# A Perceiver kernel: nine key chunks of the third cross-attention made in the stages ahead of it, kept in DRAM and reloaded

## What is computed

```
k_raw = ctx @ wk_x[g].T                       # 6272 x 128
k     = layernorm(k_raw) * w + b              # mean and variance over the 128
p     = softmax(q[g] @ k.T / sqrt(128))
mix   = p @ ctx                               # 64 x 256 for each head
out   = mix @ wv_x[g].T
```

## Time and profile before

| | |
|---|---|
| median of 3 runs | 1033.47 us (1030.02 to 1033.73) |
| span of the profiled execution | 1029.9 us |
| its own time | not on the page; the lowest run is 1030.02 us |
| PE, DVE, ACT, POOL busy | 981.5, 715.1, 359.1, 162.3 us |
| mean granted TensorE clock | 0.991 |
| HBM read, written | 62.54 MB, 0.07 MB |

### The profile page before, as it was taken

One profiled execution on the slowest core, in us unless ns is written; L12 is line 12 of the kernel. 1 busy time (PEld: TensorE's weight loads), 2 busy tenths in 40 slices (PEclk: granted clock), 3 DMA queues, 4 the chain that ended last, 5 costly groups with the idle time before them and its releaser, 6 DMA issues.

```text
span 1029.9 us, 20637 instructions
## 1 busy us (share of the span) xinstructions
PE 981.5 (95%) x7832; PEld 655.9 (64%) x7848; DVE 715.1 (69%) x1916; ACT 359.1 (35%) x629; POOL 162.3 (16%) x146
## 2 busy tenths in 40 slices
PE   9999999998799888999999999999999999898998
PEld 5676677675335444566777777777777777744555
DVE  5767767768799845886676867667676867843444
ACT  2333333334338832432333332433333332302211
POOL 0000000000210010342223223222332323000000
PEclk9999999999999999999999999999999999898999
DMA  8001001002239996940000000000000000232440
GB/s 311 25 22 42 21 20 38 23 5 84 73 115 195 190 337 250 338 170 1 1 1 1 1 0 0 0 0 0 0 0 0 0 1 2 82 144 82 159 192 4
DMA packets 66410, 75.41 MB, mean 73 GB/s; under 512 B 49329, under 2 KB 57265, under 8 KB 62513
## 3 DMA queue, kind: packets, MB, share of 16 engines
q1 hardware_dynamic: 66064, 74.57, 23.7%
q10 hardware_dynamic: 288, 0.07, 0.0%
HBM read 62.54 MB, written 0.07 MB: 61 GB/s over the span
## 4 chain that ended last, share of the span: by engine, by line
PE 77%; DVE 8%; issue 6%; DMA 3%; POOL 2%; ACT 2%; SPq 0%; POOLq 0%; DVEq 0%; PEld 0%; PEldq 0%
PE ps L2377 17%; PE ps L2271 15%; PE ps L2367 8%; PE ps L1570 8%; PE ps L1560 4%; PE ps L1581 4%; PE ps L1604 2%; PE ps L1616 2%; POOL x_sum L2902 1%; PE ps L515 1%; DVE vals L2097 1%; PE ps L2989 1%; PE ps L2294 1%; DMA wide<-vals 1%; PE ps L1590 1%
## 5 line engine op out<-in xcount | busy, mean ns | idle before, releaser
L2377 PE MATMUL ps<-vals,S 128*128 128x257 f32 x784 | 188.3, 384 | 0.7 <-ACT S L2834 0.7
L2271 PE MATMUL ps<-keysT,row_biases_sb 128*128 128x512 f32 (+1 forms) x416 | 185.4, 572 | 0.1
L2902 POOL TENSOR_TENSOR x_sum<-x_max,consts 128x4 f32<-128x4 f32 (+1 forms) x104 | 135.3, 1301 | 316.2 <-DVE x_max L2570 316.2
L2582 DVE SCALAR_TENSOR_TENSOR S<-ps,x_sum,keysT 128x128 f32<-128x128 f32 x392 | 110.9, 345 | 66.4 <-PE ps L2377 61.8
L2377 PEld LDWEIGHTS ps<-vals,S 128*128 128x128 f32 x784 | 143.1, 192 | 18.9 <-issue 1.0
L2834 ACT ACTIVATE S<-S 128x512 f32<-128x512 f32 (+1 forms) x104 | 62.6, 605 | 219.8 <-DVE S L2623 219.3
L2367 PE MATMUL ps<-x_q,x_keys 128*128 128x128 f32 x784 | 113.2, 286 | 0.0
L2271 PEld LDWEIGHTS ps<-keysT,row_biases_sb 128*128 128x128 f32 x416 | 75.9, 191 | 56.9 <-issue 51.0
L2367 PEld LDWEIGHTS ps<-x_q,x_keys 128*128 128x128 f32 x784 | 95.6, 191 | 0.1
L1570 PE MATMUL ps<-ring,S 128*128 128x512 f32 x196 | 92.3, 593 | 0.1
L2766 ACT COPY x_keys<-ps 128x512 f32<-128x512 f32 (+1 forms) x104 | 57.0, 548 | 65.4 <-PE ps L2367 32.8
(11 more groups left out here) (474 smaller groups left out, 1374.6 us busy)
## 6 DMA issues: line engine op xcount, KB each, us to landing
ring<-weights SPq DMA_DIRECT2D x24, 1024.0 KB, 7.0
keysT<-ctxT SPq DMA_DIRECT2D x2, 3136.0 KB, 14.9
vals<-ctxN SPq DMA_DIRECT2D x1, 6272.0 KB, 27.0
S<-ctxT SPq DMA_DIRECT2D x11, 512.0 KB, 4.0
ring<-weights SPq DMA_DIRECT2D x5, 768.0 KB, 5.9
keysT<-weights SPq DMA_DIRECT2D x1, 1792.0 KB, 8.9
keysT<-weights SPq DMA_DIRECT2D x1, 1536.0 KB, 12.1
row_biases_sb<-row_biases SPq DMA_DIRECT2D x1, 1416.0 KB, 9.4
```

Of the source, the lines that this page charges most:

```text
L2271: ins = pe.matmul(ps[:, x2_key_bank(g, c), 0:width(c)], x2_wk[:, k, :], ctxT[:, k, span(c)], start=k == 0, stop=k == KT - 1)
L2377: ins = pe.matmul(bank(6, D + 1), S[:, a:a + TILE], ctx_and_ones[:, SUB * c + s, :], start=c == 0 and s == 0, stop=c == NC - 1 and s == su ...
L2582: ins = dve.scalar_tensor_tensor(S[:, a:a + TILE], ps[:, 3 + c % 2, 128 * s:128 * s + 128], x2_inv[:, c % 2, s:s + 1], x2_tile_const, ALU. ...
L2902: pool.tensor_tensor(x2_inv[:, c % 2, 0:n], x2_var[:, c % 2, 0:n], C("neg_half").broadcast_to([128, n]), ALU.pow)\
```

## The change

`KEPT` names nine chunks of 512 tokens: chunks 3, 5, 7, 9 and 11 of group 1 and 3, 5, 7 and 9 of group 7. Their raw keys are made before stage 6, each as four pieces (`keep(pe, n)` issues n pieces; a piece is one f32 matmul over 256 columns, two records), and the pieces take the places of the dummy matmuls in x0 to f1. ScalarE copies a finished chunk to a free part of the tile `S` (`copy_kept`), SyncE stores it to a DRAM tensor (`store_kept`, 256 KB) and brings it back in stage 6 (`load_kept`) into the slot of `x2_keys` where the copy of stage 6 put it. Eight of the nine take their context from five extra loads of 512 KB (`load_kept_ctx`) into `x2_keys` and `x2_probsT`, which are free then; the ninth takes it from `ctxT`. The key weights of both groups are loaded early into the end of ring slot 2, and VectorE centres them in the sweep (`centre_kept_weights`).

```diff
+KEPT = ((1, 3), (GROUPS - 1, 3), (1, 5), (GROUPS - 1, 5), (1, 7), (GROUPS - 1, 7), (1, 9), (GROUPS - 1, 9), (1, 11))
+KEPT_LOADS = ((0, 3), (1, 5), (0, 7), (1, 9), (1, 9))
+KEPT_LOAD_OF = (0, 0, 1, 1, 2, 2, 3, 4, None)
+KEPT_LOAD_DONE = (0, 0, 2, 4, 7)
...
+        def keep(pe, n):
+            for piece in range(kept_pieces[0], kept_pieces[0] + n):
+                u, (half, k) = piece // 4, divmod(piece % 4, KT)
...
+                if piece % 4 == 0:
...
+                    if u >= 2:
+                        pe.wait_ge(sem("kept_copied"), since("kept_copied", u))
+                    if load is None:
+                        pe.wait_ge(sem("ctxT_in"), 16 * KT)
+                    else:
+                        pe.wait_ge(sem(f"kept_ctx{KEPT_LOADS[load][0]}"), since(f"kept_ctx{KEPT_LOADS[load][0]}", 16 * kept_load_no(load)))
...
+                ins = pe.matmul(ps[:, KEPT_BANK[u], a:a + TWO], kept_weights[:, KEPT_GROUPS.index(g), k, :], source,
+                                start=k == 0, stop=k == KT - 1)
...
+        def copy_kept(act, u):
+            if kept_units:
+                act.wait_ge(sem("kept_psum"), since("kept_psum", u + 1))
...
+                act.copy(scratch(KEPT_AT[u], CHUNK), bank(KEPT_BANK[u])).then_inc(sem("kept_copied"), 1)
+        def centre_kept_weights(dve):
...
+            link(dve, "dve", dve.tensor_reduce(mean, kept_weights_flat, AX, ALU.add))
+            link(dve, "dve", dve.tensor_scalar(mean, mean, 1.0 / GD, None, ALU.mult))
+            dve.tensor_tensor(kept_weights_flat, kept_weights_flat, spread(mean, 2, GD), ALU.subtract).then_inc(sem("kept_weights"), 1)
...
+        KEPT_NORM = {1: 4, 2: 4, 3: 4, 4: 3, 5: 4} if kept_units else {}
...
-            if n in BUSY_NORM:
+            if n in KEPT_NORM:
+                keep(pe, KEPT_NORM[n])
+            elif n in BUSY_NORM:
                 busy(pe, *BUSY_NORM[n])
```

SyncE's order gains, in the first loads, two weight loads and two context loads ahead of the sweep's own context loads, and in `load`:

```diff
+                if name == "f0_up":
+                    store_kept(sp, 0)
+                    load_kept_ctx(sp, 2)
+                    store_kept(sp, 1)
+                if name == "f0_routed":
+                    store_kept(sp, 2)
+                    load_kept_ctx(sp, 3)
+                    store_kept(sp, 3)
+                if name == "f0_down":
+                    store_kept(sp, 4)
                 if name == "f1_lora":
+                    store_kept(sp, 5)
+                    store_kept(sp, 6)
...
+                    if kept_units:
+                        sp.wait_ge(sem("x1_scores_psum"), since("x1_scores_psum", PARTS * PAIRS))
+                    load_kept_ctx(sp, 4)
                     reload_ctxT(sp)
+                if name == "f1_experts0":
+                    store_kept(sp, 7)
                 if name == "f1_experts3" and runs(6):
...
+                    store_kept(sp, 8)
+                if name == "x2_proj1" and kept_units:
+                    kept_stored(sp, len(kept_units))
+                    sp.wait_ge(sem("x2_first_in"), 16)
+                    for u in kept_order:
+                        load_kept(sp, u)
```

In stage 6 a kept chunk has no `keys`, and its scores wait for the reload. The reload waits for the scores of the chunk that used the slot before. ScalarE skips the copy, squares from `x2_keys` and does so behind the exponential:

```diff
+        def load_kept(sp, u):
+            g, c = kept_units[u]
+            sp.wait_ge(sem("x2_scores_psum"), since("x2_scores_psum", g * NC + (c - 1)))
+            sp.dma_start(x2_keys[:, c % 2, :], kept_keys[u]).then_inc(sem("x2_kept_in"), 16)
...
-                        if c + 3 < NC:
+                        if c + 3 < NC and not kept(scored, c + 3):
                             keys(scored, c + 3)
...
-                    if scored is not None and c + 2 < NC:
+                    ahead_kept = scored is not None and c + 2 < NC and kept(scored, c + 2)
+                    if scored is not None and c + 2 < NC and not ahead_kept:
                         copy_keys(scored, c + 2)
                         square(scored, c + 2)
                     if weighed is not None and c + 2 < NC:
                         exp(weighed, c + 2)
+                    if ahead_kept:
+                        square(scored, c + 2)
```

More of the change, by code:

```diff
@@ L521, in perceiver @@
         transposed_no = {n: k for k, n in enumerate(transposed)}
+        kept_units = KEPT if first == 0 and last >= 6 else ()
+        kept_order = sorted(range(len(kept_units)), key=lambda u: kept_units[u])
+        kept_keys = nc.dram_tensor("kept_keys", (len(KEPT), 128, CHUNK), F32).ap()
+        kept_weights = ring[:, 2, SLOT - 512:SLOT].rearrange("p (g k n) -> p g k n", g=2, k=KT)
+        kept_weights_flat = cut(ring[:, 2, SLOT - 512:SLOT], 4, GD)
+        kept_ctx = [cut(x2_keys[:, :, :].rearrange("p a n -> p (a n)"), KT, CHUNK),
+                    cut(x2_probsT[:, :, :].rearrange("p a n -> p (a n)"), KT, CHUNK)]
@@ new lines, in kept_stored, with load_kept_ctx @@
+        def kept_stored(eng, units):
+            for s in range(2):
+                n = len([u for u in range(units) if u % 2 == s])
+                eng.wait_ge(sem(f"kept_stored{s}"), since(f"kept_stored{s}", 16 * n))
+        def load_kept_ctx(sp, i):
+            if kept_units:
+                place, c = KEPT_LOADS[i]
+                if i >= 2:
+                    sp.wait_ge(sem("kept_psum"), since("kept_psum", KEPT_LOAD_DONE[i]))
+                sp.dma_start(kept_ctx[place], io["ctxT"][:, :, span(c)]).then_inc(sem(f"kept_ctx{place}"), 16)
@@ L603, in out_tensor @@
             k = outs.index(s)
-            if s in BUSY_OUT:
+            if s == 0 and kept_units:
+                keep(pe, 4)
+            elif s in BUSY_OUT:
                 busy(pe, *BUSY_OUT[s])
@@ L705, in mha_tensor @@
             if s in mha_by_rows:
-                busy(pe, BUSY_MHA[s][0], 4)
+                if s == 4 and kept_units:
+                    keep(pe, 1)
+                    busy(pe, BUSY_MHA[s][0] - 2, 4)
+                else:
+                    busy(pe, BUSY_MHA[s][0], 4)
                 pe.wait_ge(sem("mha_qk_ready"), mha_by_rows.index(s) + 1)
@@ L722, in mha_tensor @@
             for c in range(2):
-                if not meanwhile:
+                if s == 1 and kept_units:
+                    keep(pe, 2)
+                elif not meanwhile:
                     busy(pe, BUSY_MHA[s][2], 4)
@@ L1795, in sweep_vector @@
                         norm_vector(dve, 0)
+                if i == 1 and kept_units:
+                    centre_kept_weights(dve)
             pair_step(2 * (NC - 1), 0, subs(NC - 1))
@@ L1840, in x0_tensor, with while_waiting @@
         def x0_tensor(pe):
-            busy(pe, 2, 3)
+            def while_waiting():
+                if kept_units:
+                    keep(pe, 1)
+                else:
+                    busy(pe, 2, 3)
+            while_waiting()
             norm_tensor(pe, 0)
-            busy(pe, 2, 3)
+            while_waiting()
             normT_here(pe, 0)
@@ L1978, in x1_tensor @@
             ins.then_inc(sem("x1_q_psum"), 1)
-            busy(pe, 9, 3)
+            if kept_units:
+                keep(pe, 4)
+            else:
+                busy(pe, 9, 3)
             for i in range(2):
@@ L2133, in x1_vector @@
             for b in range(PARTS):
+                if b == 1 and kept_units:
+                    kept_stored(dve, 6)
+                if b == PARTS - 1 and kept_units:
+                    kept_stored(dve, 7)
                 score(0, b)
@@ L2354, in scores @@
             def scores(g, c):
-                pe.wait_ge(sem("x2_keys_ready"), g * NC + (c + 1))
+                if kept(g, c):
+                    kept_here(pe, g, c)
+                else:
+                    pe.wait_ge(sem("x2_keys_ready"), g * NC + (c + 1 - not_made(g, c)))
                 if c == 0:
@@ L3165, in _ @@
             sp.dma_start(filter_sb[:, :], io["filterT"]).then_inc(sem("params_in"), 16)
+            if kept_units:
+                sp.wait_ge(sem("key_weights_in"), 16)
+                sp.wait_ge(sem("vk_weights_in"), 16)
+                first_key = piece_from["x2_kx"]
+                for i, g in enumerate(KEPT_GROUPS):
+                    of_group = cut(io["weights"][:, first_key:first_key + KT * 1024], KT, 1024)[:, :, g * GD:g * GD + GD]
+                    sp.dma_start(kept_weights[:, i, :, :], of_group).then_inc(sem("kept_weights_in"), 16)
+                for i in range(2):
+                    load_kept_ctx(sp, i)
             if sweep:
```

78 lines of the change are left out of this document (72 added, 6 removed).

## The result

The changed kernel takes 1022.87 us (median of 4 runs, 1022.58 to 1027.49) against 1033.01 in 4 runs of the kernel before beside it: ratio 0.9918, 95% interval 0.9892 to 0.9943. A second series gave 1022.95 (6 runs, 1021.04 to 1024.76) against 1032.75 (11 runs): 0.9902, 0.9886 to 0.9917. The forecast was 1024.9, in a range of 1017.5 to 1032.5. A ratio is of all runs of a series and not the quotient of the two medians, which is 0.9902 and 0.9905 here: by the first ratio the change saves 8.5 us, by the second 10.1.

A forecast was written before the change was run, and what follows sets the result against it. TensorE was taken to bound the kernel, with 77% of the chain of waits. Savings of 4.2 and 4.5 us in two steps less 0.1 made 8.6 off 1033.47: 1024.9 us, range 1017.5 to 1032.5.

The forecast's parts named there:

- What comes off: Steps of groups 1 and 7: nine chunks lose key matmuls of 1.72 us each, at most 15.5 us off.
- What is late next: Kept chunks' variances wait for ScalarE's square behind the exp, then VectorE's low half: seven stalls of 0.78 us, one of 1.25.
- The steps: Third cross-attention, net of stalls: group 1's step saves 4.2 us and group 7's 4.5, together 8.8.
- The reloads: Kept keys' 256 KB loads in stage 6: taken as 3.5 us against 5.6 us of cover, so hidden, 0 us.
- The short stages: Making pieces replace dummy matmuls where TensorE waits: up to 0.1 us, ahead of the second self-attention's norm.
- its own mark: Start of the x2 stage: the forecast is wrong if it starts over 1 us later than at 406.
- sign of 0.5 us up to there: Stages up to 406 us: they were to keep their length to 0.5 us.
- The total: Whole kernel: 8.6 us off the median of 1033.47, giving 1024.9 us.
- everything comes off: Rival, 12%: in the kept steps the variance is not late, 15.5 us off, 1018.0 us.
- Making places late: Rival, 15%: a piece holds TensorE in the short stages, at the 4 us bound 4.6 us off, 1028.9 us.
- The clock: Rival, 5%: TensorE's pauses drop the clock once in each kept step, 1.8 us off, 1031.7 us.
- Late reloads: Rival, 8%: nine reloads at 6.9 us each land 1.3 beyond their cover, 3.1 us slower, 1036.6 us.

The follow-up runs named there:

- square-first kernel: Changed kernel with ScalarE taking a kept chunk's square ahead of the exp: 1018.74 us, ratio 0.9849 to the kernel before; run again, 1018.14 us, 0.9848.
- making alone: Changed kernel with nine chunks made and stored but none reloaded, stage 6 making all keys: 1033.01 us, 1.0004 to before; again 1033.06 us, 1.0003.
- late reload: Changed kernel with the trigger of each kept chunk's reload waiting for one chunk's scores more: 1042.27 us, ratio 1.0083 to the kernel before.

## Why the prediction was right, and where it was not

- **What comes off**: nine key chunks at 1.72 us. Right: the square-first kernel, where nothing stalls, has a pair at 7.56, so 9.28 - 7.56 = 1.72, and group 1's step lost 8.53 of the forecast 8.60.
- **What is late next**: seven gaps of 0.78 and one of 1.25, ended by VectorE's low half. Right in place, count and releaser. The trace shows them as 0.64 and 1.19, counted from the modelled end of `weigh`; a pair lost 0.80 (8.36 against 7.56), as forecast. The mechanism (ScalarE's square behind the exp) is shown by the exchange of the two instructions. The statement from the Trainium skill (TensorE: Matmul & The Clock Gate, Architectural detail) that these engines work strictly in order was what made it foreseeable. The traces agree: in the changed kernel ScalarE sat idle for 5.62 us ahead of the exp at 484.56, and the square behind it, whose keys were asked for at 479.6 and took 3.7 us at most, ran only at 485.09.
- **The steps**: 4.2 and 4.5 forecast, 4.05 and 4.30 measured.
- **The reloads**: hidden, right; 3.5 us was too much, 2.6 measured. From the page alone: the Trainium skill (SBUF — State Buffer, The DMA setup-cost knee) gives about 2 us plus the bytes over 436 GB/s, which makes an estimate of 2.6 us for 256 KB; this trace agrees with 2.6 there in the median (2.5 to 3.7); for the sweep's 512 KB the same rule gives an estimate of 3.2, and the row says 4.0.
- **The short stages**: 0.1 was forecast, 0.3 and 0.4 (ratios) to 0.6 (profiles) is what was measured. The place named for the 0.1, the norm of the second self-attention, is where 0.2 of it arose, and the term was mis-sized for the 0.15 us by which the pieces start later than dummies did. That f1 grows by 0.4 was missed. By its own mark (x2 over 1 us later than at 406) the forecast was in doubt in the one profile, +1.10, and its sign of 0.5 us up to there was not met. Of the 1.10, a1 and f1 are 0.40, which repeats; the other 0.70 lies ahead of them, where the three profiles of the kernel before differ by more: 273.95 to 276.33 us to f0, 100.55 to 101.55 from there.
- **Late stages**: 0 forecast, -2.0 in the profile. They vary by 7 us between two profiles of one kernel, the making alone (146.3 and 153.3).
- **The total**: the terms measure 8.35 - 0.3 to 0.6, some 7.9 us where the sum had 8.6, and yet the median came 2.0 us below the forecast. 0.5 of that is the start of the sum: 1033.47 was the median of three runs, and beside the changed kernel it was 1033.01. The rest is no term of the forecast, and that it came out so near is in part luck. (The span of 1029.9 is also not that of the run of 1030.02: in the result a run's time lies 1.8 us above its span, 1022.58 against 1020.8. No term hangs on it.)
- **The rivals**: everything comes off, no, but one exchange of two instructions makes it real (15.4 us in the two steps). Making places late, at most 0.6 and not 4. The clock, no: it was 1.00 in the kept step of group 1 with pauses of 0.64 in 8.36 us, and fell only with the late reload, where they were 2.3 to 2.6 us. What the Trainium skill (TensorE: Matmul & The Clock Gate, HAM oscillation) describes is a stream whose waits for transfers are longer than the work between them; the pauses of the changed kernel are not that case, and no fall occurred behind them. Those of the late reload, 2.3 to 2.6 in every 10 us, are not either, and yet it fell behind three of sixteen. Late reloads, no: 2.5 to 3.7 against 6.6.

The steps give -8.35 and the making +0.3 to +0.6, so about -7.9, where the medians say -10.1 and -9.8, and the second interval (8.6 to 11.8 us) leaves 7.9 just outside. The clock on record with each run closes most of this. An estimate of what the clock took from a run is its span times what its mean granted clock lacks to 1.00 (rough, since the clock is on record to 0.001, about 1 us, and runs scatter by some 2 us around each mean; the four first runs of the kernel before have no clock on record):

| kernel | runs | mean span, us | by the clock | without it |
|---|---|---|---|---|
| before | 42 | 1030.5 | 10.6 | 1019.9 |
| making alone | 21 | 1031.0 | 10.9 | 1020.1 |
| changed | 10 | 1021.5 | 9.7 | 1011.8 |
| late reload | 4 | 1040.1 | 14.3 | 1025.8 |

Without it the change saves 8.2 us and the making costs 0.1 to 0.2, near the traces' 7.9 and 0.6, and the late reload costs 14.0, near the 14.2 of its waits. The runs of the changed kernel lost 0.9 us less to the clock than those of before, the four with the late reload 3.7 more. What stays open: the late stages' mean is 1.1 us lower in the profiles with the making, in a scatter too wide to show it, and whether the changed kernel's ten runs lost less to the clock by chance alone.

## What to carry to other kernels

When matmuls are removed from a loop that TensorE fills, follow the inputs of its next instruction back through the in-order engines before the gain is booked: here half of it was lost to one square placed behind one exp. An instruction that waits for a transfer may stand ahead of one that waits for something later still; compare when each input arrives, not how risky its source seems. A late transfer can cost twice, by the wait and by the clock that falls behind it (14.2 and 3.4 us here). And price work moved into short stages by many runs, and by several profiles of both kernels, not by one pair, since one pair said 1.3 us where 0.3 to 0.6 was so.

## What was not expected of the hardware

The granted clock falls after the same stretch of short matmuls in every profile but two. In those two the eight matmuls behind it take 3.70 us, in the other eleven 4.87 to 6.49, all of them the same instructions.

The first norm of the program came at 46.8 to 49.7 us without any relation to the kernel. It is not the loads alone that differ. The first f32 matmuls start when the first context load has landed, at 4.6 to 5.9 us, and the same eight take 1.96 us in the quickest profile and 3.75 in the slowest, though the granted clock reads 1.00 over them in both. The kernel before, in its first and its second profile:

```profile
5.35 1.97 PE L1560 MATMUL ps<-S,ring 128*128 128x256 f32 x8 [0.72 <-DMA S<-ctxT]
```
```profile
5.51 3.75 PE L1560 MATMUL ps<-S,ring 128*128 128x256 f32 x8 [0.81 <-DMA S<-ctxT]
```
